# Second attention layer of a two-layer gated model: softmax weights kept keys-first, values in four column tiles

## The reference

```
lat = layernorm(latents) * w + b;  ctx = layernorm(context) * w + b
q = lat @ Wq;  k, v = split(ctx @ Wkv)            # 16 heads of 64
attn = softmax(clip(q k^T / 8, -11, 11), axis=-1)
out = (attn v) @ Wo + bo                          # Wo is 1024 x 256
```

## Time and profile before

| | us |
|---|---|
| median of 3 runs | 2055.89 (2054.28 to 2055.92) |
| the profiled execution | 2056.65 |
| its span, first to last instruction | 2054.9 |
| mean granted PE clock over the span | 0.956 of full |
| busy: PE / DVE / ACT / POOL | 1825.4 / 1279.4 / 998.6 / 606.4 |
| attention 1 with its start and its drain, about | 903 to 1625 |

### The profile page before, as it was taken

One profiled execution on the slowest core, in us unless ns is written; L12 is line 12 of the kernel. 1 busy time (PEld: TensorE's weight loads), 2 busy tenths in 40 slices (PEclk: granted clock), 3 DMA queues, 4 the chain that ended last, 5 costly groups with the idle time before them and its releaser, 6 DMA issues. The chain is left out here.

```text
span 2054.9 us, 45028 instructions
## 1 busy us (share of the span) xinstructions
PE 1825.4 (89%) x15107; PEld 1662.2 (81%) x15107; DVE 1279.4 (62%) x4134; ACT 998.6 (49%) x2468; POOL 606.4 (30%) x730
## 2 busy tenths in 40 slices
PE   5999999999996499967999999999998389999991
PEld 5899999899995488856988878888887289999990
DVE  2577777777777233335777777877877344554545
ACT  3777777777774133324545545545554133333320
POOL 0013223223223200024243434333431354445420
PEclk9999999999998699988999999999999689999995
DMA  6688011011000599972222111111110242222106
GB/s 203 236 272 290 27 37 41 26 37 39 26 25 28 163 291 290 292 240 78 83 97 71 48 47 44 45 38 45 48 38 12 68 158 91 88 79 83 52 32 251
DMA packets 134002, 213.60 MB, mean 104 GB/s; under 512 B 16767, under 2 KB 84898, under 8 KB 133841
## 3 DMA queue, kind: packets, MB, share of 16 engines
q1 hardware_dynamic: 106448, 147.89, 21.6%
q0 software_dynamic: 23040, 59.58, 9.2%
q10 hardware_dynamic: 4352, 4.20, 0.6%
HBM read 111.88 MB, written 103.68 MB: 105 GB/s over the span
## 5 line engine op out<-in xcount | busy, mean ns | idle before, releaser
L500 POOL DMA_INDIRECT buf<-a_rxn,a_disp x192 | 197.4, 1028 | 252.0 <-DVE a_disp L894 90.1
L633 ACT ACTIVATE a_S<-a_S,a_mn 128x128 f32<-128x128 f32 x512 | 198.9, 395 | 45.7 <-DVE a_mn L923 45.7
L906 DVE TENSOR_TENSOR a_S<-a_S,a_rz 128x512 f32<-128x512 f32 x256 | 177.3, 693 | 8.8
L81 PE MATMUL e_psH<-e_x_hi,e_w_hi 128*128 128x256 f32 x640 | 182.8, 286 | 0.0
L82 PE MATMUL e_psH<-e_x_lo,e_w_hi 128*128 128x256 f32 x640 | 179.6, 281 | 0.0
L83 PE MATMUL e_psH<-e_x_hi,e_w_lo 128*128 128x256 f32 x640 | 179.4, 280 | 0.0
L81 PE MATMUL a_psP<-a_c_hi,a_wk_hi 128*128 128x256 f32 x512 | 156.2, 305 | 9.3 <-DVE a_c_lo L782 9.3
L81 PE MATMUL a_psP<-a_x_hi,a_wq_hi 128*128 128x256 f32 x512 | 156.7, 306 | 5.2 <-DVE a_x_lo L782 5.2
L1132 PE MATMUL a_psT<-ident,a_S 128*128 128x128 f32 x1024 | 138.8, 275 | 17.8 <-DVE a_S L906 17.8
L1121 PE MATMUL a_psS<-a_kT,a_qT 64*128 64x128 f32 x2048 | 151.1, 288 | 3.1 <-ACT a_qT L618 1.6
L1145 PE MATMUL a_psV<-a_PT,a_v 128*64 128x128 f32 x2048 | 140.3, 279 | 8.5 <-DVE a_o_lo L937 7.0
(11 more groups left out here) (195 smaller groups left out, 5300.1 us busy)
## 6 DMA issues: line engine op xcount, KB each, us to landing
buf<-a_zeros SPq DMA_DIRECT2D x16, 1320.0 KB
buf<-a_zeros SPq DMA_DIRECT2D x16, 1024.0 KB, 6.2
e_rows<-buf SPq DMA_DIRECT2D x64, 256.0 KB, 4.0
e_w_in<-in_L_ffn_w SPq DMA_DIRECT2D x64, 256.0 KB, 3.3
y<-e_y SPq DMA_DIRECT2D x64, 256.0 KB, 3.1
a_ctx<-in_ctx SPq DMA_DIRECT2D x32, 256.0 KB
e_w_out<-in_L_ffn_w SPq DMA_DIRECT2D x64, 128.0 KB, 3.9
y<-a_zeros SPq DMA_DIRECT2D x32, 256.0 KB
```

The costliest lines, as they stand in the source:

```text
L81: pe.matmul(dst, a_hi, b_hi, start=start, stop=False)
L500: g_.indirect_dma_start(out=buf, out_offset=bass.IndirectOffsetOnAxis(ap=disp[:, par, i, k:k + 1], axis=0), in_=rxn[:, par, i], in_offset= ...
L633: ins = a.activation(s[:, h], s[:, h], ACT.Exp, bias=mn[:, u % 2, h:h + 1], scale=-1.0, accum_out=z[:, u % 2, h:h + 1])
L906: v_.tensor_tensor(s, s, rz[:, (u - 1) % 2, :].unsqueeze(2).broadcast_to([P, HU, P]), ALU.mult).then_inc(s_norm, 1)
```

## The change

Only layer 1 changes. The scores are computed with the operands exchanged, so that keys stand on partitions and queries run along the free dimension. The exponentials then have the layout that the product with the values needs, and `invert`, `turn_probs` and `evac_probs` are no longer called. `weigh_turned` multiplies, per unit, four heads by three parts: the two halves of 32 columns of the values, and a 128x32 tile of ones. The head `j` of the unit goes to the column tile `32*j`. The part with the ones gives the sums over the keys, repeated on 32 partitions. The new DVE function `heads` inverts these sums (128x128 per unit, read from PSUM) and multiplies the heads by them into `o_all`; ACT rounds `o_all` to `oT` (`heads_hi`), and DVE takes the rest as `o_lo` (`heads_lo`). The output projection becomes three products of rounded halves. Its weights, loaded by eight DMAs in the new order of rows, wait for the place of the raw values' weights and are split before the first step by ACT (`wo_hi`) and DVE (`w_out_lo`).

```diff
-                     if not first:
-                         v_.tensor_reduce(z[:, (u - 1) % 2], s, AX, ALU.add).then_inc(s_rz, 1)
-                         ve.wait_ge(s_rz, at(g, RZ * UG, RZ * u - 1))
...
+            def heads(g, w):
+                u = 2 * w
+                if has(g, u, 4):
+                    half = (w - 2) % 2
+                    ve.wait_ge(s_pv, at(g, UG, u - 2))
+                    for e in range(2):
+                        ins = v_.reciprocal(rzb[:, e], psO[e][:, 2])
+                    ins.then_inc(s_rz, 1)
+                    ve.wait_ge(s_rz, at(g, UG // 2, w - 1))
+                    for e in range(2):
+                        ins = v_.tensor_tensor(o_all[:].rearrange("p (h u) q -> p h u q", h=2)[:, :, 2 * half + e], psO[e][:, 0:2],
+                                               rzb[:, e].unsqueeze(1).broadcast_to([P, 2, P]), ALU.mult)
+                    ins.then_inc(s_op, 1)
...
             def heads_lo(g, w):
                 u = 2 * w
-                if first and has(g, u, 4):
+                if has(g, u, 4):
+                    ve.wait_ge(s_oT, at(g, UG // 2, w - 1))
+                    v_.tensor_tensor(parts(o_lo, w), psV[:] if first else parts(o_all, w), parts(oT, w).bitcast(F32),
+                                     ALU.subtract).then_inc(s_ol, 1)
...
# DVE, step
-                invert(g, 2 * w)
+                if first:
+                    invert(g, 2 * w)
+                else:
+                    heads(g, w)
                 read_scores(g, 2 * w)
...
                 read_scores(g, 2 * w + 1)
                 heads_lo(g, w)
-                invert(g, 2 * w + 1)
+                if first:
+                    invert(g, 2 * w + 1)
...
# ACT
+            def heads_hi(g, w):
+                u = 2 * w
+                if has(g, u, 4):
+                    act.wait_ge(s_op, at(g, UG // 2, w - 1))
+                    if not isinstance(g, int) or g * UG + u >= 8:
+                        act.wait_ge(s_wo, at(g, GT, (u - 4) // 4))
+                    a.activation(parts(oT, w), parts(o_all, w), ACT.Copy).then_inc(s_oT, 1)
...
             def step(g, w, par, proj, prep):
-                evac_heads(g, w)
+                if first:
+                    evac_heads(g, w)
+                else:
+                    heads_hi(g, w)
...
# PE
+            def weigh_turned(g, u, par):
+                if has(g, u, 2):
+                    pe.wait_ge(s_exp, at(g, UG, u - 1))
+                    un = (u - 2) % UG
+                    vpar = par if u >= 2 else 1 - par
+                    if u % 2 == 0 and has(g, u, 4):
+                        pe.wait_ge(s_op, at(g, UG // 2, u // 2 - 1))
+                    for part in range(3):
+                        for j in range(HU):
+                            i, odd = divmod(j, 2)
+                            col = ((un % UT) * HU + j) * DH + part * HQ
+                            left = ones[:] if part == 2 else v[:, vpar, un // UT, col:col + HQ]
+                            ins = mm(psO[u % 2][j * HQ:(j + 1) * HQ, part], left, S[:, (u - 2) % 4, 2 * odd + i],
+                                     start=True, stop=True)
+                    ins.then_inc(s_pv, 1)
...
             def project_out(g, w, proj, prep):
-                    pe.wait_ge(s_ol if first else s_oT, at(g, UG // 2, 4 * i // 2 + 2))
+                    pe.wait_ge(s_ol, at(g, UG // 2, 4 * i // 2 + 2))
...
                     for c in range(HP):
-                        if first:
-                            ins = split_product(nc.tensor, psM[:, 0], oT[:, c], o_lo[:, c], wo_hi[:, c], wo_lo[:, c],
-                                                c == 0, c == HP - 1)
-                        else:
-                            ins = mm(psM[:, 0], oT[:, c], wo[:, c], start=c == 0, stop=c == HP - 1)
+                        ins = split_product(nc.tensor, psM[:, 0], oT[:, c], o_lo[:, c], wo_hi[:, c], wo_lo[:, c],
+                                            c == 0, c == HP - 1)
...
# SP
-            if not first:
-                sp.dma_start(wo[:], d["L1_xattn_Wo"].rearrange("(c p) n -> p c n", p=P)).then_inc(s_late, 16)
+            sp.wait_ge(s_w["v"], 18)
...
+                src = d["L1_xattn_Wo"].rearrange("(u j h d) n -> j h d u n", u=UT, j=HU, h=2)
+                for j in range(HU):
+                    for h in range(2):
+                        sp.dma_start(raw_wo[j * HQ:(j + 1) * HQ, h * UT:(h + 1) * UT], src[j, h]).then_inc(s_late, 16)
```

More of the change, by code:

```diff
@@ L38 @@
 HU = 4
+HQ = P // HU
 UT = H // HU
@@ L328, in attention, with parts @@
         block = stack.enter_context(nc.Block())
+        LATE_ALL = 32 if first else 16 * (2 * HU + 1)
+        def parts(ap, w):
+            half = (w - 2) % 2
+            if first:
+                return ap[:, half * 4:half * 4 + 4]
+            return ap[:].rearrange("p (h u) q -> p h u q", h=2)[:, :, 2 * half:2 * half + 2]
         JOBS = [("k", i) for i in range(4)] + [("v", i) for i in range(4)] + [("q", i) for i in range(4)]
@@ L609, in evac_job @@
                     act.wait_ge(s_sc, at(g, WG, -WG))
-                if first and g == 1 and j == 8:
+                if g == 1 and j == 8:
                     act.wait_ge(s_wos, 2)
@@ L913, in read_scores @@
                     if has(g, u, 4):
-                        ve.wait_ge(s_tr, at(g, UG, u - 3))
+                        ve.wait_ge(s_tr if first else s_pv, at(g, UG, u - 3))
                     ve.wait_ge(s_sc, at(g, WG, u // 2 + 1))
@@ L1042, in before @@
                 inputs(1)
+                w_out_lo()
             run(ve, step, before)
@@ L1140, in weigh_values @@
                     if u % 2 == 0 and has(g, u, 4):
-                        pe.wait_ge(s_ol if first else s_oT, at(g, UG // 2, u // 2 - 1))
+                        pe.wait_ge(s_ol, at(g, UG // 2, u // 2 - 1))
                     for i in range(2):
@@ L1199, in step @@
                 project_out(g, w, proj, prep)
-                weigh_values(g, 2 * w, par)
-                weigh_values(g, 2 * w + 1, par)
+                weigh = weigh_values if first else weigh_turned
+                weigh(g, 2 * w, par)
+                weigh(g, 2 * w + 1, par)
             def router_inputs(g, par):
@@ L1233, in before @@
             def before():
+                if not first:
+                    pe.wait_ge(s_rwz, 3)
                 transpose_ctx(0)
```

81 lines of the change are left out of this document (42 added, 39 removed).

## The result

The changed kernel takes 2069.05 us (2066.61 to 2074.83) where the kernel before takes 2055.89: ratio 1.0071, 95% interval 1.0060 to 1.0083. It is 0.7% slower; the forecast was 0.7% faster. The profiled execution is one of 2069.05 us, 12.4 us above that of before.

What follows compares the result with a forecast made beforehand. DVE's list was taken to bound layer 1 at 41.1 us a group: 13 x 1.4 = 18 us less, 1 + 3 us more, 14 less than 2056.65; against the median 2042 us, own range 2033 to 2051, full range 2024 to 2076.

Steps and rivals of the forecast that it cites:

- DVE as the bound: Attention in layer 1: DVE's list, not PE's, sets the pace of 41.1 us a group.
- the prices: New DVE instructions: reciprocal of 128x128 0.95 us, product of 128x256 0.416 us, subtraction of 128x512 0.684 us.
- The pace: DVE's time per group in layer 1: 39.7 us after the change for 41.1 before, 1.4 us less.
- Rivals 3 and 4: DVE's reciprocal: at 1.2 us, 2068 us, chance 0.11; at 0.31 us, PE takes over, 2016 us, chance 0.07.
- four column tiles overlap: PE's weighing: four tiles take half the time of two, 0.032 us an instruction, 1.5 us a step.
- Rival 2: PE's weighing: four column tiles no faster than two, 3.1 us a step; 2103 us, chance 0.15.
- The part on PE: PE's work per group in layer 1 falls from 38.6 to 36.0 us, hidden under DVE's 39.7.
- Rival 1: PE's idle pieces in steps 2 and 3 lower its clock, 1.5 us a group; 2062 us, chance 0.17.
- a granted clock of 1.00 in the stage: PE in attention of layer 1: the clock stays at full speed after the change.
- the prediction's own sign of being wrong: PE in attention of layer 1: a granted clock below 0.95 would show the prediction wrong.
- the drain: Last groups of layer 1: `update_x` waits for the projection up to 2.4 us, none to four times; +3 us.
- The start: Start of layer 1: `w_out_lo` stands ahead of a norm that waits for POOL anyway; +1 us, 2.3 at worst.

Runs made afterwards that it cites:

- e5: Kernel before with only the output projection of the second layer split into three products of rounded halves, with its subtraction on DVE: 2083.88 us, ratio 1.0148.
- e13: Changed kernel, all four engine lists of the second layer written out, 8 unused products in step 3 from the second group on: 2045.09 us.
- e11: Kernel before with the lists of PE, DVE, ACT and POOL of the second layer written out instead of looped: 2047.72 us, ratio 0.9971.
- e1: Changed kernel with PE's list of the second layer written out, other engines still looped: 2058.24 us, ratio 1.0012 to the kernel before.
- e7: Kernel before with PE's list of the second layer written out, other engines still looped: 2053.42 us, ratio 1.0003.
- e12: Changed kernel, PE's list written out, 8 unused products a group in step 3, 16 and 12 more in the last groups: 2054.17 us.
- e9: Changed kernel with the lists of PE, DVE, ACT and POOL of the second layer written out: 2050.12 us, ratio 0.9984 to the kernel before.
- e3: Changed kernel, loops kept, with 8 unused products of 512 columns ahead of step 3's third projection job, first group included: 2067.33 us.
- e6: Changed kernel with PE's list written out and 8 unused products in step 3 from the second group on: 2057.15 us, ratio 1.0015.
- e14: Changed kernel, loops kept, PE's weighing of step 3 written at the next group's head, so the jump follows the output projection: 2062.08 us.

## Why the prediction was wrong

**Right: DVE as the bound, and the prices.** In e5 more work on DVE and less on PE made the groups longer. The reciprocal is 0.920 us for 0.95, product and subtraction as in the earlier trace rows. The pace is 39.57 and 40.12 us in the first intervals, and 479.6 / 12 = 40.0 in e13 without jumps and falls of the clock, for 39.7. Against 41.2 in e11 the gain is 1.3 us a group; forecast was 1.4. Rivals 3 and 4 fall with this. That DVE alone still sets the pace after the change is not shown: in e13 PE is busy 97% of the time, spare products included.

**Right: four column tiles overlap.** 48 instructions start within 1.24 us of the first, 0.026 us each (16 from 1187.37, 8 from 1187.83, and the same again from 1188.05); 1.5 us was forecast, with a lower bound of 1.44 that proved too high. Rival 2 is out.

**Failed: the loop's end, which the sum has at nothing.** The part on PE priced the added instructions by their time alone (48 for 24 a step, 24 for 16 a projection) and took PE's saving as hidden under DVE; it did not ask what 898 matmuls for 674 do to a loop body. Before, PE's jump takes 0.21 us, and no `issue` stands among PE's waits in the view of the earlier trace rows; now it takes 3.5 to 3.8 us, and the 1.25 us of weighing that stand last hide little of it. Price: 11.4 us (e1), none before (e7). That the long instructions had covered the same jump before, as e1 and e7 put it, is not borne out. A sign that a jump can cost time stood in the kernel before: DVE's standstills of 7.8 us.

**Failed: the chance of Rival 1.** It had 0.17, and "a granted clock of 1.00 in the stage" was forecast; from 1100 us on it was 0.93 to 0.98, past the prediction's own sign of being wrong (below 0.95). The mechanism is as described, an idle piece of 2.3 to 2.6 us in step 3 (forecast 2.8) and the clock behind it in two groups of three, at 0.6 us a group. That 2069 lies near this rival's 2062 is luck: its clock is 6.9 of the 26.4 us that were missed.

**Failed: the drain, a term mis-sized.** +3 was forecast, up to 2.4 us for each of four waits, and +12.0 came. The step priced only the wait for the projection at full clock; PE stood ahead of it, the clock was down behind that (4.7 us by e12), and both halves of the change lengthen the chain.

**The start** was put at +1 us and is at -3.1. Most of this is no effect: with nothing altered ahead of the layer's steps, e7 and e11 start the second group at 1031.5 and 1032.6.

**The sum.** The twelve intervals were forecast at 502.0 - 12 x 1.4 = 485.2 us and took 506.9, 21.7 more: PE's jump 11.4 (after less e1), the clock 6.9 (e9 less e13), the other engines' loops 1.8 (they cost 495.5 - 486.5 = 9.0 now, 502.0 - 494.8 = 7.2 before), the pace 1.7 ((1.4 - 1.26) x 12). With the drain's 9.0 more, the thirteenth group's 1.4, the start's 4.1 less and the rest's 1.4 less, that is 26.6 us; the time missed is 2069.05 - 2042.65 = 26.4. These shares depend on the order in which things are taken away: the spare products took 8.0 us off the twelve intervals with all loops in place (e3) and 2.8 with PE's list alone written out (e6).

## What to carry to other kernels

A change that puts more instructions into a loop body can make the jump at its end dear, however short they are: look there for a standstill without a releaser, and for transfers of instructions that the loop did not have. Writing the list out took the cost away here (e1); turning the loop so that longer work stands ahead of the jump hid half of it (e14). Time saved on an engine that is not the bound comes back as idle pieces, and on PE these can lower the clock for the very work that others wait for. A drain has no other work to hide under: price a longer chain there at its full length, and at the lower clock.

## What the runs showed of the hardware that was not expected

- The jump: 0.21 us on PE in the kernel before and in e5, 3.4 to 5.0 us in every looped kernel with column tiles, where the trace also has transfers of instructions on PE's queue in the loop. It shows as 3.2 to 3.5 us of standstill behind 1.25 us of short products and up to 2.0 behind 2.9 us of longer ones (e14). The looped lists of DVE, ACT and POOL cost 7.2 us in three jumps in the kernel before (502.0 - 494.8).
- Column tiles of 32: 0.026 us from start to start, in bursts of 48 at full clock. Of the two floors in the Trainium skill, "TensorE: Matmul & The Clock Gate", section "Wait — 56ns, not 53.3ns?", this trace rules out the one of 62 ns; it lies at the one of about 25. Whether that floor is what bounds the burst is not shown: in the drain, at the lower clock, the same instructions follow each other by 0.053 us (16 from 1591.21 to 1592.06).
- Lists written out cost nothing that shows, though PE's then needs 13 transfers of instructions in 200 us (e7): no `issue` stands among PE's waits there, and the kernel before gained 0.3% with all four lists written out (e11).
